# Statistics transfers and one softmax broadcast issued by ScalarE, with a new order of small steps on ScalarE and VectorE

## The reference

```
xn   = (x - mean_group) / sqrt(var_group + 1e-5)         # 32 groups of 12 channels
w    = xn^T @ qkv_w^T                                    # (pixels, 384), head h owns 32 columns
s    = sum over a head's columns of w*w / (sum over pixels of w*w)
Pi   = softmax over heads of (s * temp)
Pi_n = Pi / (sum over pixels of Pi + 1e-8)
dots = sum over pixels of Pi_n * w*w
out  = -(w * Pi) / (1 + dots)
y    = x + out @ out_w^T + out_b
```

## Time and profile before

| | us |
|---|---|
| median of 3 runs (lowest, highest) | 910.02 (908.90, 911.25) |
| the profiled execution | 909.34 |
| its span | 907.6 |
| PE busy in the span | 861.0 |
| DVE busy | 743.8 |
| ACT busy | 523.4 |
| POOL busy | 225.6 |

### The profile page before, as it was taken

The page is one execution under the profiler, slowest core; times in us unless marked ns, Lnnn a source line. Parts: engine busy times, 40 slices in busy tenths (PEclk is TensorE's granted clock), DMA queues, the critical chain, the costliest instruction groups (busy, mean ns, idle before and its releaser), DMA issues.

```text
span 907.6 us, 14234 instructions
## 1 busy us (share of the span) xinstructions
PE 861.0 (95%) x4322; PEld 687.0 (76%) x4322; DVE 743.8 (82%) x1368; ACT 523.4 (58%) x676; POOL 225.6 (25%) x101
## 2 busy tenths in 40 slices
PE   7799999999999999999999999999999999999996
PEld 6577787777777777778777778777778777778785
DVE  7588888888888888888888888888888888888755
ACT  4566555667555667555667655567655567655621
POOL 1331133332123332123332123333123333113300
PEclk9899999999999999999999999999999999999998
DMA  7314664544665544565544565544565444464432
GB/s 286 123 46 177 216 217 154 183 143 172 214 216 165 176 144 169 211 216 175 184 142 167 197 216 188 175 148 163 192 216 203 161 160 165 179 215 148 145 120 93
DMA packets 54852, 158.47 MB, mean 175 GB/s; under 512 B 21426, under 2 KB 25778, under 8 KB 50866
## 3 DMA queue, kind: packets, MB, share of 16 engines
q1 hardware_dynamic: 54688, 158.25, 51.5%
q10 hardware_dynamic: 146, 0.00, 0.0%
HBM read 105.70 MB, written 52.53 MB: 174 GB/s over the span
## 4 chain that ended last, share of the span: by engine, by line
PE 50%; DMA 16%; issue 13%; DVE 11%; ACT 7%; SPq 2%; ACTq 1%; DVEq 0%
PE acc L482 46%; DMA PIB<-pi 12%; DMA pi<-PIT 4%; PE scores L562 3%; DVE WV L778 3%; ACT WS L386 2%; ACT XH L414 2%; ACT WV L395 1%; DVE UL L788 1%; SPq L301 1%; SPq L296 1%; ACT UH L376 1%; PE acc L465 1%; DVE WS L752 1%; DVE PIT L740 1%
## 5 line engine op out<-in xcount | busy, mean ns | idle before, releaser
L336 POOL TENSOR_TENSOR XL<-XN,XH 128x1024 fp32r<-128x1024 f32 x93 | 222.6, 2408 | 617.2 <-ACT XH L414 616.2
L386 ACT ACTIVATE WS<-acc 128x1024 f32<-128x1024 f32 x96 | 97.6, 1017 | 236.2 <-PE acc L482 177.5
L482 PE MATMUL acc<-UH,W2H 128*128 128x512 f32 x576 | 179.1, 392 | 4.5 <-ACT UH L376 4.5
L482 PE MATMUL acc<-XH,W1H 128*128 128x512 f32 x576 | 178.7, 392 | 3.7 <-ACT XH L414 3.7
L482 PE MATMUL acc<-UH,W2L 128*128 128x512 f32 x576 | 178.4, 391 | 0.0
L482 PE MATMUL acc<-XH,W1L 128*128 128x512 f32 x576 | 178.2, 391 | 0.0
L796 DVE SCALAR_TENSOR_TENSOR X<-acc,bias,X 128x1024 f32<-128x1024 f32 x96 | 120.1, 1276 | 56.9 <-PE acc L482 56.8
L376 ACT ACTIVATE UH<-WV 128x1024 fp32r<-128x1024 f32 x96 | 98.1, 1054 | 108.6 <-DVE WV L778 108.3
L482 PE MATMUL acc<-UL,W2H 128*128 128x512 f32 x576 | 150.2, 396 | 0.0
L482 PE MATMUL acc<-XL,W1H 128*128 128x512 f32 x576 | 147.0, 391 | 0.0
L752 DVE CUSTOM_DVE_ANT_0 WS<-PIB,WS 128x1024 f32<-128x1024 f32 x96 | 117.2, 1223 | 23.3 <-DMA PIB<-pi 21.7
(11 more groups left out here) (78 smaller groups left out, 443.2 us busy)
## 6 DMA issues: line engine op xcount, KB each, us to landing
PIB<-pi SPq DMA_DIRECT2D x96, 528.0 KB, 6.0
out_y<-X SPq DMA_DIRECT2D x96, 512.0 KB, 6.8
X<-in_x SPq DMA_DIRECT2D x31, 1536.0 KB, 6.2
gathered<-stats_rows SPq DMA_DIRECT2D x31, 72.0 KB, 2.8
pi<-PIT SPq DMA_DIRECT2D x96, 16.5 KB
X<-in_x SPq DMA_DIRECT2D x3, 512.0 KB, 4.5
WV<-in_L_conv_qkv_w SPq DMA_DIRECT2D x1, 576.0 KB, 6.4
WS<-in_L_conv_out_w SPq DMA_DIRECT2D x1, 576.0 KB, 7.4
```

What stands on the lines that cost most here:

```text
L336: pool.tensor_tensor(XL[:, t, :], XN[:, t, :], XH[:, t, :].bitcast(F32), ALU.subtract).then_inc(xl_done, 1)
L386: act.activation(square_tile(i, t), acc[:, t, :], ACT.Square, accum_out=sumsq[:, t:t + 1]).then_inc(squared, 1)
L482: last = pe.matmul(out[:, h * BANK:(h + 1) * BANK], w[:, k, m * P:(m + 1) * P], r[:, k, h * BANK:(h + 1) * BANK], start=(n == 0 and k == 0 ...
```

## The change

Four things are changed. First, the write and the read back of the statistics of images 2 and later move from SP's program to the end of ACT's step. The first ones, of image 1, stay on SP. Second, the third of the three softmax broadcasts (tile 2) is issued by ACT, between `normalise(2)` and `x_hi(2)`, and no longer by SP. Third, ACT makes the seed (`group_seeds`) right behind `u_hi(0)` in every step from 1 on; in step 0 it moves ahead of `keep_w(1)`. Fourth, on DVE `group_norm` moves ahead of the three `u_lo`, and `head_sum_weights` between the second and the third of them. In the last step `finish(i-2, 2)` moves behind the three `weigh`, and at the start the statistics of image 1 are taken before the low parts of the second weight matrix.

```diff
             def step(i):
                 store(i - 2, 2)
                 ...
                 spread_pi(i)
-                write_stats(i + 2)
                 store(i - 1, 0)
                 store(i - 1, 1)
-                gather_stats(i + 2)
-
-            write_stats(FIRST + 1)
-            gather_stats(FIRST + 1)
+
+            write_stats(sp, FIRST + 1)
+            gather_stats(sp, FIRST + 1)
...
-                    for t in range(T):
+                    for t in range(T - 1):
                         sp.wait_ge(pi_written[t], j.counts(16, 16))
...
                 u_hi(0)
+                if i.follows(1):
+                    group_seeds(i + 1)
                 square_w(1)
                 u_hi(1)
                 u_hi(2)
                 square_w(2)
+                if has(i) and not i.follows(1):
+                    group_seeds(i + 1)
                 keep_w(1)
-                if has(i):
-                    group_seeds(i + 1)
                 keep_w(2)
...
                 normalise(2)
+                if has(i):
+                    act.wait_ge(pi_written[T - 1], i.counts(16, 16))
+                    act.dma_start(PIB[:, T - 1].rearrange("p b n -> p (b n)"), spread_rows(T - 1))\
+                        .then_inc(pi_spread[T - 1], 16)
                 x_hi(2)
+                if i.follows(0):
+                    write_stats(act, i + 2)
+                    gather_stats(act, i + 2)
...
-                if not has(i) and has(i - 1):
-                    finish(i - 2, 2)
                 for k in range(4):
                     attention(i - 1, k)
                 group_moments(i + 1)
                 weigh(i - 1, 0)
                 weigh(i - 1, 1)
                 weigh(i - 1, 2)
+                if not has(i) and has(i - 1):
+                    finish(i - 2, 2)
+                group_norm(i + 1)
                 u_lo(i - 1, 0)
                 u_lo(i - 1, 1)
+                head_sum_weights(i)
                 u_lo(i - 1, 2)
-                head_sum_weights(i)
-                group_norm(i + 1)
                 group_stats(i + 2, [0])
...
+            group_stats(FIRST + 1, range(T))
             weights_lower(range(T, 2 * T))
...
-            group_stats(FIRST + 1, range(T))
             pipeline(dve, step, 0, B + 1)
```

More of the change, by code:

```diff
@@ L223, in norm_of, with spread_rows @@
             return norm[:, j.slot % 2, 0:1], norm[:, j.slot % 2, 1:2]
+        def spread_rows(t):
+            return pi_dram[t * HPT:(t + 1) * HPT].unsqueeze(0).to_broadcast([D, HPT, BLOCKS * QUADS * (QUAD + 1)])
         def w_tile(j, t):
@@ L234, in x_tile, with write_stats, gather_stats @@
             return X[:, j.slot, t * N:(t + 1) * N]
+        def write_stats(eng, j):
+            if has(j):
+                eng.wait_ge(gn_step, j.counts(GN_STEPS, GN_MEASURED))
+                if j.follows(2):
+                    eng.wait_ge(stats_gathered, j.counts(16, -16))
+                eng.dma_start(stats_dram, stats[:].rearrange("p k s -> p (k s)")).then_inc(stats_written, 16)
+        def gather_stats(eng, j):
+            if has(j):
+                eng.wait_ge(gn_step, j.counts(GN_STEPS, GN_AGGREGATED - GN_STEPS))
+                eng.wait_ge(stats_written, j.counts(16))
+                rows = stats_dram.rearrange("(g k) s -> g (k s)", k=PER_GROUP).unsqueeze(1)
+                eng.dma_start(gathered[:], rows.to_broadcast([GROUPS, PER_GROUP, PER_GROUP * T * HALVES * 6]))\
+                        .then_inc(stats_gathered, 16)
         def pipeline(eng, step, first, last):
@@ L264, in _ @@
                 load(Image(j, j))
[L266 to L281, removed]
             def store(j, t):
@@ L296, in spread_pi @@
                         sp.dma_start(rows, PIT[:, t, :]).then_inc(pi_written[t], 16)
-                    for t in range(T):
+                    for t in range(T - 1):
                         sp.wait_ge(pi_written[t], j.counts(16, 16))
-                        heads = pi_dram[t * HPT:(t + 1) * HPT].unsqueeze(0)\
-                            .to_broadcast([D, HPT, BLOCKS * QUADS * (QUAD + 1)])
-                        sp.dma_start(PIB[:, t].rearrange("p b n -> p (b n)"), heads).then_inc(pi_spread[t], 16)
+                        sp.dma_start(PIB[:, t].rearrange("p b n -> p (b n)"), spread_rows(t)).then_inc(pi_spread[t], 16)
             def step(i):
```

## The result

The changed kernel takes 951.9 us (median of 4 runs, 950.8 to 953.4) against 910.6 us of the kernel before (4 runs, 908.9 to 913.7) on the same chip. The ratio is 1.045, with a 95% interval of 1.042 to 1.048. It is slower by 41 us; the forecast was 14 us faster. The result also lies outside the range.

The account below looks back on a forecast made before the run. TensorE nearly full, but a ring of dependences sets 27.08 us an image; 25.74 plus 0.9 gives 26.64, saving 12.3 us over 28 periods plus 0.6 in the last step: forecast 896 us, range 880 to 920.

Parts of the forecast that it names:

- PE's floor: Head sums to head sums: PE itself needs 26.14 us an image; reaching this was a rival at 882 to 884, chance 0.20.
- the ring: Dependences from head sums through softmax, broadcasts, `dot`, statistics, `weigh` and `u_lo` to the next head sums: 27.07 us an image.
- g: Before DVE's aggregation of the gathered statistics: the part of the old wait that is left, 0 to 1.2 us.
- x and g do not add: In the period's sum: a late `dot` gives the statistics time, so only the longer term counts, taken as 0.9 us.
- x: At the last `dot`: shift from issuing tile 2's broadcast on ACT's queue, -0.2 to 1.3 us.
- 25.74 us: The period between head sums without x and g: 27.07 less 1.20 (statistics' wait) less 0.13 (exponential).
- slow stretch: During the broadcasts, 446.0 to 448.4 us: only 116 to 222 GB/s, costing about 1.5 us, which two queues might fill.
- Rival C: ACT's small statistics transfers fall behind SP's stores: read back 1.3 us later, 943 us in all; chance 0.20 with D.
- D: ACT waits for the statistics' write before `square_w(0)`: no cost unless it lands after 452; counted into Rival C.
- PE's wait: PE's idle time before the head sums: to shrink from 0.9 us in an image to about 0.5.
- The exchange of the seed, `group_norm` and head sum weights: Reordering around `u_lo` ahead of and behind the head sum weights: to cancel within 0.05 us.
- the exponential's 0.13: On ACT after the maximum is subtracted: the exponential no longer starts late, winning 0.13 us a period.

Follow-up runs that it names:

- e6_stats_act_hold: Changed kernel with tile 2's broadcast back on SP's queue and SP's two stores held until it has landed: 880.6 us, 0.967 of the kernel before.
- e13_write_first: Changed kernel with one exchange on ACT: the statistics' write is issued before tile 2's broadcast, not behind it: 907.8 us, 0.997 of the kernel before.
- e4_hold_stores: Changed kernel with SP's two stores held until tile 2's broadcast has landed: 884.4 us, 0.973 of the kernel before.
- e2_stats_act: Changed kernel with tile 2's broadcast back on SP's queue, the statistics staying on ACT's: 895.3 us, 0.984 of the kernel before.
- e5_before_hold: Kernel before, with the statistics' read back ahead of the two stores and the stores held until tile 2's broadcast has landed: 891.8 us, 0.979.
- e7_moves_only: Kernel before with both transfers (tile 2's broadcast, the statistics) on ACT's queue and none of the new orders: 961.3 us, 1.055.
- e9_old_start: e6_stats_act_hold with the start's order as in the kernel before: 879.1 us, 0.966 of the kernel before.
- e3_pib_act: Changed kernel with the statistics back on SP's queue, tile 2's broadcast staying on ACT's: 904.9 us, 0.995 of the kernel before.
- e8_hold_longer: Changed kernel with SP's two stores held until the statistics have been read back: 937.5 us, 1.030 of the kernel before.
- e12_hold_tile1: Changed kernel with SP's two stores held until tile 1's broadcast has landed: 912.0 us, 1.001 of the kernel before.

## Why the prediction was wrong, point by point

**The frame was right.** PE's floor is 26.14 us a period: e6_stats_act_hold runs at 26.15. The loss is in the ring that the prediction named, and it closes in the profile after as it did before.

**The step that failed: g, which was bounded at 1.2 us, and with it "x and g do not add".** The sum started at 25.74 us and took the longer of two terms, 0.9. Measured in the image above, the last `dot` comes 16.23 us after the head sums against 15.26 - 0.13, so x is 1.10, inside its bounds. The wait left before the aggregation is 1.48. 25.74 + 1.10 + 1.48 = 28.32, the measured 28.31; that the pieces of a ring add up to it is no finding, but it shows that nothing else was lost. The prediction counted g from the head sums on, as a fixed time which a late `dot` uses up. Counted so, g is 1.10 + 1.48 = 2.58 us, more than twice its upper bound, and the longer term, which sets the ring, is g. What was wrong is that the two were taken to go on independently. ACT's queue has the write behind tile 2: whatever delays tile 2 delays the write, and then the read back.

The read back leaves 2.16 us later after the head sums than before (17.66 against 15.50). Of these, 0.97 us is tile 2, whose `dot` starts that much later; the other 1.19 is the write's own time beside the stores, which lands 1.43 us after tile 2, where it landed 0.24 after the last broadcast (taken from the starts of the last `dot` and of the read back's issue). The read back itself is 0.90 us quicker (from its issue to the aggregation 2.15 against 3.05), which leaves 1.26 for the aggregation. e13_write_first takes only the order in ACT's queue away. The aggregation then waits for nothing, while the last `dot` is about as late as in the changed kernel (16.31 us after the head sums, x = 1.18): 25.74 + 1.18 = 26.92, for a pair of head sums 26.78 us apart and a mean of 26.96.

**Why 1.2 was no bound.** "If the write is through only when the broadcasts are, as now, it lands at 450.5 and nothing is won" left out that the broadcasts themselves end later, and that the write can end well after them. The write needs 8.7 us instead of 6.4.

**x: right in size, wrong in kind.** I expected tile 2 sooner and tile 1 later. Tile 1 stays (6.2 us against 6.0) and tile 2 comes later (8.1 against 6.8). The Trainium skill ("DMA: Bandwidth & Descriptors", "Queues, rings and completion order") says that the engines take turns between queues that have work. Here two broadcasts issued 1 us apart on two queues show no turns (0.01 MB on ACT's queue until 469 us, 4 us after its issue). It is the same with the stores held: in e4_hold_stores tile 2 is issued at 460.16 us, and until 463.5 only SP's queue moves data, 0.96 MB from 460 on. Tile 2 and the stores do share, 0.27 MB to 0.11 and then 0.19 to 0.23. Why the first is so stays open. The section "Issuing engines are not separate DMA queues" says that a second issuing engine saves only issue time. The measured times differ: in e2_stats_act the write is issued 0.28 us after the first broadcast instead of 2.04, and besides it lands in 4.1 us instead of 6.4. What counted was which transfer stood behind which.

**The stores.** I noted that they move forward "into the time in which the statistics pass" and gave them no price. This was the costly sentence. e4_hold_stores takes them out of the time of tile 2 and wins 67.5 us, more than the whole loss, since they already cost the kernel before its slow stretch (e5_before_hold). I took the 116 to 222 GB/s of the earlier trace rows for something that transfers would fill or not fill; nothing in the views I read said that the stores made it, and asking what else was outstanding in that stretch would have raised it.

**Rival C was right in direction, with 0.20, and near in price by luck.** Its price was 943 us, its read back lands 19.8 us after the head sums (454.8 less 435.03), and it lands there: issued at 17.66, 2.1 us long. The composition was off. C gave 0.65 us to the write and 0.65 to the read back, for turns of small pieces with the stores. The write lost 1.19, the read back won 0.90, and the rest is tile 2, which C mentioned without counting it. The order in ACT's queue, which made 44 us, C did not name. C's test, "period is above 27.1 us and the aggregation waits for more than 1.2 us", is met: 28.51, and 48.4 us in 30 images.

**D** costs nothing, but not for the reason given. It was to cost something once the write lands after 452, which is 17 us after the head sums, and the write lands at 17.66. `square_w(0)` starts 18.44 us after the head sums instead of 15.54, and ACT still has 1.30 us to spare before UH (2.94), because `weigh` is later too.

**PE's wait.** The prediction expected 0.5 us before the head sums in an image; it is 0.79 (23.8 in 30), hardly less than the 0.9 before. That PE would come to stand still for UH, 38.3 us in all, it did not name.

**The small terms.** The exchange of the seed, `group_norm` and head sum weights cancels: 7.79 against 7.80 us. The first broadcast is issued 7.01 us after the head sums, before 7.16: the exponential's 0.13. The end gives 1.1 us, forecast 0.6. The start, counted as 0, costs 2.7 us. With the orders alone it is 1.9, but with the moves alone, in the start's old order, it is 3.5 (e7_moves_only, third head sums at 86.59 us), so both have a part in it. With the stores held, e9_old_start, which puts the old order back, has it gone.

**The chances.** I held 0.68 for a gain beyond the noise against 0.20 for C. With one of the two moves alone a gain is what came: e2_stats_act and e3_pib_act are both faster than before, though e3_pib_act only through the new orders. What I did not ask is what the two parts do to each other in one queue.

## What to carry to other kernels

A small transfer on which a chain depends goes ahead of the big one in its queue; swapping these two issues was worth 44 us here, with stores running beside them. Bulk stores that nobody waits for are held until the transfers that somebody waits for have landed (15 us won in e6_stats_act_hold, 19 in e5_before_hold, where the read back moved too, 67 in e4_hold_stores), but not until the next load is late (e8_hold_longer lost 53 of the 67 us again), and in this kernel a second queue was no protection from them. When the transfers behind two terms of a sum stand in one queue, the delay of the first is part of the second, and neither can be bounded alone.

## What the runs showed of the hardware that I had not expected

Stores slow broadcasts even when they stand behind them in the same queue: the last one lands in 6.8 us with stores issued, in 5.9 with stores held. By what means is open.

A 72 KB read back takes 2.2 us with the stores held until it has landed (e8_hold_longer), 3.0 when issued together with stores (e4_hold_stores) or while broadcasts run and stores are held (e6_stats_act_hold), 4.3 when it follows stores by 1.2 us (e12_hold_tile1), and 6.5 to 6.6 when broadcasts and stores are both on their way (e13_write_first, e2_stats_act). The 18 KB write takes 4.0 us with nothing before it in its queue (e6_stats_act_hold), 5.3 behind a broadcast with the stores held (e4_hold_stores), and 8.7 behind a broadcast and beside stores (the changed kernel).
